# Position bias: weight split, first logarithms and first bias tiles moved across two stage borders

## The reference

```python
kv = _grid_sample(xn, vgrid_scaled)           # sampled at learned offsets, 8x8 per group
k, v = _gconv1x1(kv, kw), _gconv1x1(kv, vw)
pos = grid_q[:, :, None, :] - grid_kv[:, None, :, :]
bias = jnp.sign(pos) * jnp.log1p(jnp.abs(pos))
bias = jax.nn.relu(bias @ cpb_w1 + cpb_b1)    # 2 -> 128
bias = jax.nn.relu(bias @ cpb_w2 + cpb_b2)    # 128 -> 128
bias = bias @ cpb_w3 + cpb_b3                 # 128 -> 1
attn = jax.nn.softmax(qh @ kh^T * scale + bias)
out = attn @ vh
```

## Time and profile before

| | before |
|---|---|
| median of 3 runs | 4123.54 us (4123.34 to 4124.0) |
| the profiled execution | 4125.24 us, span 4123.4 us |
| mean granted TensorE clock | 0.965 |
| TensorE matmul busy | 3823.4 us, 93% of the span |
| VectorE busy | 2983.8 us, 72% |
| ScalarE busy | 2601.1 us, 63% |
| GpSimd busy | 2103.9 us, 51% |
| sampling stage | 0 to about 107 us |
| position-bias stage | 107 to 2257 us |
| first attention product | 2260.31 us |

### The profile page before, as it was taken

The page is one execution under the profiler, slowest core; times in us unless marked ns, Lnnn a source line. Parts: engine busy times, 40 slices in busy tenths (PEclk is TensorE's granted clock), DMA queues, the critical chain, the costliest instruction groups (busy, mean ns, idle before and its releaser), DMA issues. The chain is left out here.

```text
span 4123.4 us, 67052 instructions
## 1 busy us (share of the span) xinstructions
PE 3823.4 (93%) x18640; PEld 2415.5 (59%) x18640; DVE 2983.8 (72%) x4512; ACT 2601.1 (63%) x4638; POOL 2103.9 (51%) x1933
## 2 busy tenths in 40 slices
PE   6899999999999999999999999989988737979999
PEld 3555555555555555555555788856766524845555
DVE  7888888888888888888887633364999875345554
ACT  5899999999999999999997433342221252113333
POOL 0555555555555555555554255513777731036664
PEclk8999999999999999999999999999999868989999
DMA  1200000000000000000000200025999961453312
GB/s 50 105 10 10 10 12 10 10 10 10 10 10 10 10 10 12 10 10 10 10 10 25 82 17 1 1 70 176 407 401 403 371 252 53 163 142 72 73 42 82
DMA packets 150006, 327.19 MB, mean 79 GB/s; under 512 B 44696, under 2 KB 49496, under 8 KB 149004
## 3 DMA queue, kind: packets, MB, share of 16 engines
q1 hardware_dynamic: 108364, 174.80, 13.6%
q0 software_dynamic: 41472, 151.01, 9.3%
q10 hardware_dynamic: 64, 0.02, 0.0%
HBM read 246.50 MB, written 79.04 MB: 79 GB/s over the span
## 5 line engine op out<-in xcount | busy, mean ns | idle before, releaser
L558 POOL TENSOR_TENSOR cpb_sum<-cpb_tab 128x512 f32<-128x512 f32 x1028 | 1045.7, 1049 | 965.4 <-DVE cpb_r L688 965.1
L669 ACT ACTIVATE cpb_h<-cpb_z,net_vec 128x512 f32<-128x512 f32 x1536 | 1006.1, 697 | 50.9 <-PE cpb_z L609 38.3
L606 PE MATMUL cpb_z<-cpb_r,cpb_w2a 128*128 128x512 f32 x2048 | 858.3, 419 | 23.2 <-DVE cpb_h L729 23.2
L688 DVE SCALAR_TENSOR_TENSOR cpb_r<-cpb_sum,cpb_r 128x512 fp32r<-128x512 f32 x1024 | 696.5, 711 | 187.1 <-ACT cpb_r L663 187.1
L607 PE MATMUL cpb_z<-cpb_r,cpb_w2b 128*128 128x512 f32 x2048 | 801.6, 391 | 0.0
L609 PE MATMUL cpb_z<-cpb_r,cpb_w2a 128*128 128x512 f32 x2048 | 799.8, 391 | 0.0
L688 DVE SCALAR_TENSOR_TENSOR cpb_r<-cpb_z,cpb_r 128x512 fp32r<-128x512 f32 x1028 | 662.0, 686 | 159.9 <-ACT cpb_r L663 154.3
L663 ACT ACTIVATE cpb_r<-cpb_z 128x512 fp32r<-128x512 f32 x1028 | 560.5, 604 | 128.4 <-PE cpb_z L593 128.4
L663 ACT ACTIVATE cpb_r<-cpb_sum 128x512 fp32r<-128x512 f32 x1024 | 598.3, 648 | 2.1 <-POOL cpb_sum L558 2.1
L606 PEld LDWEIGHTS cpb_z<-cpb_r,cpb_w2a 128*128 128x128 f32 x2048 | 384.0, 188 | 365.9 <-issue 300.7
L618 PE MATMUL cpb_zo<-cpb_h,cpb_w3w 128*32 128x512 f32 x3584 | 477.3, 605 | 0.0
(11 more groups left out here) (356 smaller groups left out, 5326.5 us busy)
## 6 DMA issues: line engine op xcount, KB each, us to landing
conv_out<-dc_ys SPq DMA_DIRECT2D x576, 64.0 KB
cpb_log<-log_dram SPq DMA_DIRECT2D x66, 256.0 KB, 3.1
qk_parts<-gn_r SPq DMA_DIRECT2D x64, 256.0 KB, 2.0
dc_wr<-in_dc_wT SPq DMA_DIRECT2D x9, 1024.0 KB
bias_dram<-cpb_bst SPq DMA_DIRECT2D x520, 8.0 KB
net_x<-in_x SPq DMA_DIRECT2D x8, 1024.0 KB, 11.5
sa_qa<-qk_parts SPq DMA_DIRECT2D x14, 512.0 KB
sa_ka<-qk_parts SPq DMA_DIRECT2D x14, 512.0 KB
```

The source lines that it names most:

```text
L558: pool.tensor_tensor(SUM[:, r, :].rearrange("p (y x) -> p y x", x=W), TAB[:, slot, r, 0, :].unsqueeze(1).broadcast_to([P, NF // W, W]), TA ...
L606: pe.matmul(z2[:, bank, :], W2A[:], R1[:, k, :], start=True, stop=False)
L669: act.activation(H2[:, t % 8, :], z2[:, t % 3, :], ACT.Relu, bias=V("cpb_b2")).then_inc(h2a, 1)
L688: v.scalar_tensor_tensor(R2[:, t % RING, :], first_layer(t), 0.0, R1[:, t % RING, :].bitcast(F32), ALU.max, ALU.subtract).then_inc(r2_read ...
```

## The change

Four things move, and the computation is the same.

- The load of W2F, its split into W2A and W2B, the zeroing of W3W (GpSimd, behind its other fills) and W3W's eight columns go to the sampling stage. VectorE's part stands between `hats(0, 1)` and the wait for the logarithm.
- The first load of the logarithms goes to SyncE's end of the sampling stage. The tiles W2A, W2B, W3W and LOG are kept on the right side of memory; placeholders of their sizes keep the bias stage's other tiles at their addresses.
- The copy of the sampled values to KV stands ahead of the two axis masks on VectorE, and KBD's scaling is done by ScalarE.
- The first three bias tiles are loaded inside the bias stage, behind the loop's last logarithm load and ahead of the last stores. `BS` is kept on the right side for that.

```diff
@@ layer0_sampling, sync
             sp.dma_start(W1F[:], d["w1rows"]).then_inc(w_in, 16)
+            sp.dma_start(W2F[:], d["cpb_w2"]).then_inc(w2_in, 16)
...
             sp.wait_ge(log_out, 16 * 16)
+            g["logs"](sp, slice(0, 1))
@@ gpsimd
             pool.memset(VBD[:], 0.0).then_inc(zeroed, 1)
+            pool.memset(W3W[:], 0.0).then_inc(zeroed, 1)
@@ scalar
+            act.wait_ge(zeroed, 5)
+            act.wait_ge(k_mm, 1)
+            for gh in range(2):
+                r = slice(gh * DH, gh * DH + DH)
+                act.activation(KBD[r, :, gh * NJ:(gh + 1) * NJ], po[r, :].rearrange("p (a j) -> p a j", j=NJ),
+                               ACT.Copy, scale=DH ** -0.5).then_inc(kbd_ready, 1)
@@ vector
             hats(0, 1)
+            v.wait_ge(w2_in, 16)
+            v.tensor_copy(W2A[:], W2F[:]).then_inc(split, 1)
+            v.wait_ge(split, 1)
+            v.tensor_tensor(W2D[:], W2F[:], W2A[:].bitcast(F32), ALU.subtract).then_inc(split, 1)
+            v.wait_ge(split, 2)
+            v.tensor_copy(W2B[:], W2D[:]).then_inc(split, 1)
+            v.wait_ge(zeroed, 6)
+            for c in range(8):
+                v.tensor_copy(W3W[:, c, c:c + 1], V("cpb_w3")).then_inc(w3_ready, 1)
             v.wait_ge(pos_ln, 1)
...
+            v.wait_ge(zeroed, 5)
+            v.wait_ge(kv_mm, 1)
+            v.tensor_copy(KV, pk[:]).then_inc(kv_ready, 1)
+
             v.wait_ge(pos_step, n)
             v.tensor_scalar(PX[:], POS[:], V("axis_mask", 0), None, ALU.mult).then_inc(pos_step, 1)
             v.wait_ge(pos_step, n + 1)
             v.tensor_scalar(POS[:], POS[:], V("axis_mask", 1), None, ALU.mult).then_inc(pos_step, 1)
-
-            v.wait_ge(zeroed, 5)
-            v.wait_ge(kv_mm, 1)
-            v.tensor_copy(KV, pk[:]).then_inc(kv_ready, 1)
-            v.wait_ge(k_mm, 1)
-            for gh in range(2):
-                r = slice(gh * DH, gh * DH + DH)
-                v.tensor_scalar(KBD[r, :, gh * NJ:(gh + 1) * NJ], po[r, :].rearrange("p (a j) -> p a j", j=NJ),
-                                DH ** -0.5, None, ALU.mult).then_inc(kbd_ready, 1)
@@ layer0_bias, sync
-            logs(slice(0, 1))
-            sp.dma_start(W2F[:], d["cpb_w2"]).then_inc(w_in, 16)
             sp.wait_ge(tables, 2)
...
+            sp.wait_ge(stored, 16 + 128 * ITERS)
+            for a in range(3):
+                g["load_bias"](sp, a)
             sp.wait_ge(staged, ITERS + 1)
             store(slice(ITERS, ITERS + 1))
@@ gpsimd
-            pool.memset(W3W[:], 0.0).then_inc(win_zero, 1)
-            pool.memset(H2[:, 4:8, :], 0.0).then_inc(win_zero, 1)
+            pool.memset(H2[:, 4:8, :], 0.0).then_inc(h2_zero, 1)
@@ tensor
-            pe.wait_ge(win_ready, 8)
-            pe.wait_ge(win_zero, 2)
+            pe.wait_ge(w3_ready, 8)
+            pe.wait_ge(h2_zero, 1)
@@ layer0_attention, sync
-            for a in range(PAIRS):
-                if a >= 3:
-                    sp.wait_ge(sim_mm, a - 2)
-                sp.dma_start(BS[:, a % 3, :], g["bias"].rearrange("(a p) n -> a p n", p=P)[a]).then_inc(bias_in[a % 3], 16)
+            for a in range(3, PAIRS):
+                sp.wait_ge(sim_mm, a - 2)
+                g["load_bias"](sp, a)
```

More of the change, by code:

```diff
@@ L125, in layer0_sampling @@
                                                        s.sem("pos_sgn"), s.sem("w1_step"))
+        W2F, W2D = s.sb("w2f", [P, P]), s.sb("w2d", [P, P])
+        W2A, W2B, W3W = g["W2A"], g["W2B"], g["W3W"]
+        split, w3_ready, w2_in = g["split"], g["w3_ready"], s.sem("w2_in")
         block = s.block()
@@ L452, in layer0_bias @@
         TPI = KPI * 2
-        W2F = s.sb("w2f", [P, P])
-        W2A, W2B = s.sb("w2a", [P, P], F32R), s.sb("w2b", [P, P], F32R)
-        W3W = s.sb("w3w", [P, 8, 32])
+        W2A, W2B, W3W = g["W2A"], g["W2B"], g["W3W"]
+        s.sb("room", [P, 3 * P + 8 * 32])
         EXP = s.sb("exp", [P, 2, NF], BF16)
@@ L459, in layer0_bias @@
         SUM = s.sb("sum", [P, 4, NF])
-        LOG, TAB = s.sb("log", [P, 2, 4, 2, W]), s.sb("tab", [P, 2, 4, 2, W])
+        LOG = g["LOG"]
+        s.sb("log_room", [P, 2, 4, 2, W])
+        TAB = s.sb("tab", [P, 2, 4, 2, W])
         H2 = s.sb("h2", [P, 8, NF])
         BST = s.sb("bst", [P, NF])
-        W2D = BST[:, 0:P]
         z1 = s.ps("z1", [P, 4, NF])
@@ L466, in layer0_bias @@
         zo = s.ps("zo", [P, NF])
-        w_in, split, win_zero, win_ready = s.sem("w_in"), s.sem("split"), s.sem("win_zero"), s.sem("win_ready")
+        split, w3_ready, h2_zero = g["split"], g["w3_ready"], s.sem("h2_zero")
         exp_ready = s.sem("exp_ready")
@@ L472, in layer0_bias @@
         h2_free = s.sem("h2_free")
-        log_in, table_step, tables, sum_ready = s.sem("log_in"), s.sem("table_step"), s.sem("tables"), s.sem("sum_ready")
+        log_in, logs = g["log_in"], g["logs"]
+        table_step, tables, sum_ready = s.sem("table_step"), s.sem("tables"), s.sem("sum_ready")
         staged = s.sem("bias_staged")
@@ L705, in _ @@
             table(1)
-            v.wait_ge(w_in, 16)
-            v.tensor_copy(W2A[:], W2F[:]).then_inc(split, 1)
-            v.wait_ge(split, 1)
-            v.tensor_tensor(W2D, W2F[:], W2A[:].bitcast(F32), ALU.subtract).then_inc(split, 1)
-            v.wait_ge(split, 2)
-            v.tensor_copy(W2B[:], W2D).then_inc(split, 1)
-            v.wait_ge(win_zero, 2)
-            for c in range(8):
-                v.tensor_copy(W3W[:, c, c:c + 1], V("cpb_w3")).then_inc(win_ready, 1)
             v.sem_inc(h2v, FREE)
@@ L743, in layer0_attention @@
         qf, af = Q[:].rearrange("p t n -> p (t n)"), AO[:].rearrange("p t n -> p (t n)")
-        BS = s.sb("bs", [P, 3, HW])
+        BS, bias_in = g["BS"], g["bias_in"]
         E = s.sb("e", [P, 3, NC * 2, NJ])
@@ L750, in layer0_attention @@
         pv = s.ps("pv", [P, 2, NF])
-        bias_in = [s.sem(f"bias_in{u}") for u in range(3)]
         sim_mm, maxed, shifted, exp_done = s.sem("sim_mm"), s.sem("maxed"), s.sem("shifted"), s.sem("exp_done")
@@ L2644, in build @@
             g["log_dram"] = nc.dram_tensor("log_dram", (GROUPS * B * NJ // KPI, 2, 4, 2, W), F32).ap()
+            g["W2A"], g["W2B"] = k.sb("w2a", [P, P], F32R, side="right"), k.sb("w2b", [P, P], F32R, side="right")
+            g["W3W"] = k.sb("w3w", [P, 8, 32], side="right")
+            g["LOG"] = k.sb("log", [P, 2, 4, 2, W], side="right")
+            g["log_in"], g["w3_ready"], g["split"] = k.sem("log_in"), k.sem("w3_ready"), k.sem("split")
+            g["logs"] = lambda sp, i: sp.dma_start(
+                g["LOG"][:], g["log_dram"][i].rearrange("o s r a x -> o (s r a x)").broadcast_to([P, 2 * 4 * 2 * W])
+                .rearrange("p (s r a x) -> p s r a x", s=2, r=4, a=2)).then_inc(g["log_in"], 16)
             layer0_sampling(nc, d, g)
+            g["BS"] = k.sb("bs", [P, 3, HW], side="right")
+            g["bias_in"] = [k.sem(f"bias_in{u}") for u in range(3)]
+            g["load_bias"] = lambda sp, a: sp.dma_start(
+                g["BS"][:, a % 3, :], g["bias"].rearrange("(a p) n -> a p n", p=P)[a]).then_inc(g["bias_in"][a % 3], 16)
             g["WO"], g["W1"] = a.sb("wo", [P, CT, C]), a.sb("w1", [P, CT, HID])
```

7 lines of the change are left out of this document (2 added, 5 removed).

## The result

The changed kernel took 4135.89 us (median of 10 runs, 4132.21 to 4139.57), the kernel before 4123.44 in the same series (10 runs, 4121.48 to 4129.2). The ratio is 1.0031, with a 95% interval of 1.0023 to 1.0039: slower by about 12.5 us, where 9.5 less was forecast and nothing above 4119 lay in the range. The profiled execution of the changed kernel took 4136.13 us with a span of 4134.3, at a mean granted clock of 0.967 (before 0.965).

The account below looks back on a forecast made before the run. TensorE was taken to bound the bias loop, with nothing hidden at its ends. Gains of 1.1 + 5.1 + 3.3 = 9.5 us from 4123.54 gave 4114.0 us, range 4111.0 to 4119.0.

Parts of the forecast that it names:

- Rival 3: Bias loop: one table instruction a turn held 0.81 us, leaving 0.44 a turn, 28 us slower in all, 4142; chance 0.05.
- The tail: End of the sampling stage: the sampled values' copy, now ahead of the masks, starts earlier; 1.1 us gained.
- The added work: Sampling stage: VectorE's three 128x128 instructions and eight column copies fit in 5.67 idle us; cost 0, uncovered 1.5.
- The prologue: Start of the bias stage: TensorE waits only for GpSimd's fill of H2, opening near 111.1; 5.1 us gained.
- Rival 1: Bias prologue: VectorE's four table instructions shut GpSimd out, fill ends 1.3 us later, gain 8.2, 4115.3; chance 0.10.
- The seam: Between bias stage and attention: the first bias tiles are requested earlier, so TensorE starts near 2257.0; 3.3 us gained.
- rival 2: Seam: last stores queue behind the bias-tile loads, leaving the seam 0.5 to 1 us, 4116.5; chance 0.12.
- The restart: TensorE's restart at attention: expected at the low clock level (1.2 GHz) again, despite shorter idle time of 5.1 us.
- The sum: Whole kernel: gains of 1.1 + 5.1 + 3.3 = 9.5 us, taken from the median 4123.54 to give 4114.0.

Follow-up runs that it names:

- the mended version: The changed kernel with a 1952-byte right-side pad and W2B ahead of W2A, putting the halves at 209984 and 209472: 4116.01 us against 4123.33, ratio 0.9984.
- the version with the copies: The changed kernel with ScalarE copying W2A and W2B back to their old addresses at the bias stage's start: 4114.8 us against 4122.64, ratio 0.9982.

## Why the prediction was wrong

**The step that failed** is in the first paragraph: "Nothing at the ends can change that", said of a loop in which TensorE is busy 494.49 of 500 us. The ends could, for they moved two operands of the loop's products. Every move of a tile was priced by what it overlaps with, and none by its address. The loop has 6144 products with W2, and 22.3 us over them, 3.6 ns for each, are more than all three gains.

**Rival 3** had the place ("W2's halves, W3W and the logarithms lie elsewhere") and a right test: it decides from 0.15 us a turn, and 0.35 were measured. It had the wrong mechanism, one table instruction of VectorE held by 0.81 us in each turn. In the changed loop VectorE does less in 500 us, not more (413.63 against 418.69), and moving the halves alone with the entry as it was brings all of the loss. Its "against it", that GpSimd's wait pins the phase, was right of the phase and said nothing of the address. So 0.05 was too little for a place that I had named and could not price: no row of before shows the same product with its weights at another address, and that is a cost unbounded from above, not one of zero.

**The tail: right, 0.93 for 1.1.** From TensorE's last sampling products to the first spread are 11.44 us before and 10.51 in the mended version (95.93 to 106.44), where the key products took 2.08 as before. The changed kernel's own trace shows 8.72, but there they took 1.16, at a granted clock of 1.00 (2.4 GHz) where it was 0.50 (1.2 GHz) before and in the mended version. That is no mark of the change: of the four profiles with the new tail one had it, and of the fourteen with the old tail seven (the run with W3W and LOG moved among them). Like against like, the old tail took 11.34 to 11.47 us at the low clock and the new one 10.51 or 10.52; at the full clock the old one took 10.2 to 10.5 and the new one 8.7. The copy follows TensorE's end by 0.1, and ScalarE's scaling took 1.21, ended at 103.14 and was waited for by nobody, as said.

**The added work: right, 0.** VectorE's eleven instructions were done at 72.52, and 4.45 us of its 5.67 idle ones are still left.

**The prologue: right, 5.2 for 5.1.** GpSimd's spreads took 2.04, its fill 1.80, and TensorE opened at 108.82, 0.15 after the fill. The mended version has the same 5.79 from spread to layer 2.

**Rival 1 did not happen,** though both engines left the barrier together. It was VectorE that was held: its table instructions end at 106.02, 108.76 and 108.83, by the ends of GpSimd's spread and fill, and the last one, after the fill, took 0.27. The Trainium skill ("SBUF — State Buffer", on engine ports) has the pair go to whichever starts first. This trace does not bear that out: VectorE's first instruction started 0.06 earlier (little to decide it by) and still was the one that took 1.19; GpSimd's spreads kept their 2.04.

**The seam: right, 3.4 for 3.3.** The loads took 5.4 to 6.8 us to land, more than the 5.5 that I used as the worst. The last, issued from 2261.96, landed at 2268.75, 1.8 us after the first store was issued at 2266.98: the condition of rival 2 was met. From the first issue to the last landing were 8.0 us, where the forecast had 6.7 (2246.3 to 2253). The block still opened in time, TensorE starting 5.03 us behind the last read-out, and 5.02 in the mended version, where the forecast had 5.1. So the cost of **rival 2 did not come,** or was less than 0.1. The restart was at the low level, 0.50 over 2271.2 to 2276.5, as forecast.

**The sum.** Tail, prologue and seam come to 0.9 + 5.2 + 3.4 = 9.5, as forecast. With the placement mended the spans differ by 10.1 us (4123.4 to 4113.3), and the medians by 7.3 (4123.33 to 4116.01) and, in the version with the copies, 7.8. The intervals of those ratios reach from some 3 to 11 us, so 9.5 lies in both. The mended version was expected at 4112 and came to 4116.01; whether 2 us are lost elsewhere can't be told from these runs. The forecast of 4114.0 was the time of a kernel that keeps its loop as it is. The changed kernel has a loop that costs 22.3 more.

## What to carry to other kernels

Where a stage is bound by TensorE and loads other weights for each product, the address of its operands is a part of the code: write down each one before and after a change, and treat one that moves as a cost of unknown size, to be measured by moving it alone. A placeholder that keeps the other tiles in place does not help the tile that was moved. When a busy engine does less in the same time, compare the starts of its instructions, line by line, before looking for a wait.

## What the runs showed of the hardware

Products of 128x512 in fp32r, each with a weight load of 128x128, started every 0.2293 us or, at distance 160, every 0.2332, depending on where the weights lay to the streamed operand within 256 bytes; the weight loads themselves took 188 ns either way. Of the distances tried, 32 and 160 cost most (0.34 a turn) and 192 least (0.10; the only one tried with R1 and R2 moved). It is not the weights' own address that counts: 128 past a multiple of 256 costs 0.30 a turn when R1 is at 64, and nothing when R1 is at 128. That distance 0 is free was seen at two places of R1; that the other costs go by the distance alone was not tried at a second place of R1. Of the products with W3W, 605 ns in every group shown, nothing of the kind was seen, also where W3W moved by 160 against H2 (67.6 ns from start to start in both). Halves at distances of less than 32 bytes were not tried.

The Trainium skill ("SBUF — State Buffer", the table of engine ports) gives TensorE two independent read ports, one for the moving operand and one for the weight loads. By it alone the two could not meet, and the turn would be 33.25 us at any distance. These runs show 33.25 to 33.60, so a product and its weights are not independent of where they lie. Why is open. That TensorE's two reads meet is the nearest reading, but ScalarE writes R1 and VectorE reads R1 and writes R2 while TensorE works, and these accesses move with R1 and R2 too; no experiment took them away. The trace speaks against either engine alone. From a tile's third product to the next tile's first, at 300 to 2200 us, the changed kernel takes 236 ns where ScalarE writes R1 through the whole step (847 steps) and 236 where it does not at all (480), before 228.3 and 229.5. With VectorE's instruction on R1 and R2 through the whole step or not at all it is 237 and 236 (621 and 169 steps), before 230 and 228. Steps free of both engines do not occur. The starts with W2A alone displaced show that a product with badly placed weights comes late; whether its load or the product running ahead of it is slowed, no run shows.
